# One block load moved ahead of a wait, zero fills cut into eight pieces, and ScalarE's first steps reordered in a fused gated-recurrence and mixture-of-experts kernel

## The reference

```python
x = x + layernorm(attn(layernorm(x)))   # gated recurrence, 4 heads of 64
x = x + layernorm(ffn(layernorm(x)))    # 16 experts, each token goes to the best 4

# attn: gates = (x @ W_in.T) @ W_gate.T + b_gate, split per head into i, f, o, c
c = sigmoid(f) * c + exp(i) * tanh(c_t)                 # scan over the 256 tokens
h = sigmoid(o) * tanh(c * rsqrt(mean(c*c) + eps) * rms_w)
y = h @ W_out.T

# ffn: logits = x @ router.T + bias; softmax over the best 4
out = sum over chosen experts: score * (((up + 1) * gate * sigmoid(1.702 * gate)) @ down_e + bias_e)
```

## Time and profile before

| | us |
|---|---|
| time before, median of 3 runs | 754.29 (753.38 to 758.72) |
| span of the profiled execution | 764.0 |
| first gates of block 0 / of block 1 on PE | 21.35 / 41.34 |
| first scatter on GpSimd | 132.51 |
| last scatter of block 5 issued | 315.58 |
| first transpose of the expert tiles | 323.13 |

### The profile page before, as it was taken

The page is one execution under the profiler, slowest core; times in us unless marked ns, Lnnn a source line. Parts: engine busy times, 40 slices in busy tenths (PEclk is TensorE's granted clock), DMA queues, the critical chain, the costliest instruction groups (busy, mean ns, idle before and its releaser), DMA issues.

```text
span 764.0 us, 13518 instructions
## 1 busy us (share of the span) xinstructions
PE 649.2 (85%) x3800; PEld 419.4 (55%) x3800; DVE 517.9 (68%) x1478; ACT 460.7 (60%) x929; POOL 392.4 (51%) x299
## 2 busy tenths in 40 slices
PE   5989999789979957398999999999999999983460
PEld 2444656465646636355666666666666666651240
DVE  3616587768858887877777777777777777730893
ACT  2676895637656545356677777777777777740242
POOL 0002223333466677646767787566666656665122
PEclk9989998979979976589999999999999999995555
DMA  7965872789532323556977677667766767745997
GB/s 246 421 264 95 166 126 38 177 297 346 175 118 97 121 93 120 151 133 108 181 162 156 124 129 123 108 106 112 112 108 102 119 99 107 111 56 70 350 178 110
DMA packets 111207, 114.86 MB, mean 150 GB/s; under 512 B 31426, under 2 KB 100818, under 8 KB 109474
## 3 DMA queue, kind: packets, MB, share of 16 engines
q0 software_dynamic: 35312, 50.22, 38.6%
q1 hardware_dynamic: 75826, 63.79, 27.9%
HBM read 54.94 MB, written 59.03 MB: 149 GB/s over the span
## 4 chain that ended last, share of the span: by engine, by line
PE 63%; DMA 14%; DVE 10%; ACT 5%; issue 5%; POOL 2%; SPq 0%; POOLq 0%; ACTq 0%; DVEq 0%
DMA routed<-arena,small 9%; PE PS L671 8%; PE PS L672 8%; PE PS L673 8%; PE PS L522 8%; PE PS L660 4%; PE PS L691 4%; PE PS L679 4%; PE PS L692 4%; PE PS L693 4%; DMA sums<-arena 3%; PE PS L555 2%; PE PS L547 2%; PE PS L531 2%; DVE small L1435 1%
## 5 line engine op out<-in xcount | busy, mean ns | idle before, releaser
L1020 POOL DMA_INDIRECT sums<-arena x143 | 223.9, 1566 | 115.6 <-DMA sums<-arena 52.3
L988 POOL DMA_INDIRECT routed<-arena,small x104 | 113.9, 1096 | 84.4 <-DMA routed<-arena,small 70.2
L1406 DVE TENSOR_SCALAR arena<-PS,small 128x256 f32<-128x256 f32 x143 | 77.8, 544 | 90.2 <-ACT arena L945 67.2
L522 PE MATMUL PS<-arena 128*128 128x512 f32 x256 | 131.8, 658 | 5.6 <-ACT arena L745 4.9
L945 ACT ACTIVATE arena<-PS,small 128x256 f32<-128x256 f32 x143 | 67.8, 474 | 99.2 <-PE PS L673 79.1
L745 ACT ACTIVATE arena<-PS 128x512 f16<-128x512 f16 (+1 forms) x179 | 104.5, 591 | 32.7 <-PE PS L500 13.0
L671 PE MATMUL PS<-W,arena 128*128 x286 | 109.4, 383 | 0.2 <-DVE arena L1408 0.2
L672 PE MATMUL PS<-W,arena 128*128 x286 | 109.4, 383 | 0.0
L673 PE MATMUL PS<-W,arena 128*128 x286 | 109.2, 382 | 0.0
L522 PEld LDWEIGHTS PS<-arena 128*128 128x128 f32 x256 | 51.2, 211 | 59.2 <-issue 56.1
L691 PE MATMUL PS<-W,arena 128*128 x286 | 78.1, 273 | 5.0 <-DVE arena L1396 4.8
(11 more groups left out here) (181 smaller groups left out, 1061.1 us busy)
## 6 DMA issues: line engine op xcount, KB each, us to landing
arena<-routed SPq DMA_DIRECT2D x143, 128.0 KB
W<-w_gu SPq DMA_DIRECT2D x8, 1024.0 KB, 23.4
W<-neg_mem POOLq DMA_DIRECT2D x16, 512.0 KB, 8.5
sums<-zero SPq DMA_DIRECT2D x2, 4096.0 KB
W<-sums SPq DMA_DIRECT2D x16, 512.0 KB, 8.8
X<-x SPq DMA_DIRECT2D x8, 512.0 KB, 4.8
W<-w_dn SPq DMA_DIRECT2D x4, 1024.0 KB, 11.3
out<-X SPq DMA_DIRECT2D x8, 512.0 KB
```

What stands on the lines that cost most here:

```text
L522: last = mm(PS[:, 2 + c % 2, :], WcT[:, k, c * P:(c + 1) * P], xT[:, k, :], start=(k == 0), stop=(k == KT - 1))
L988: pool.indirect_dma_start(routed, bass.IndirectOffsetOnAxis(ap=idx, axis=0), rows[b][:, jk // TOPK, :], None).then_inc(rows_sent[lane], 16)
L1020: pool.indirect_dma_start(sums[j % SUMS], bass.IndirectOffsetOnAxis(ap=dst[j % MU], axis=0), yb[u], None, compute_op=ALU.add).then_inc(y_s ...
L1406: L.send(v.tensor_scalar(up[j % 2], acc[:, FF:2 * FF], gu_hi, gu_lo, ALU.min, ALU.max))
```

## The change

- SyncE runs ring_x(6) together with ring_x(5), ahead of the wait for the accumulating DMAs and of the bias load.
- The two zero fills of 4 MB become eight of 1 MB (`clear(n)`), each behind a wait for a count of gate chunks: (5,5), (5,7), (6,1), (6,5), (6,7), (7,1), (7,5), (7,7). The stores of blocks 3, 4 and 5 stand between them, and the spare fills come behind the last one. GpSimd's wait counts eight fills.
- ScalarE evacuates one quarter of WcT, then normalizes block 0, then evacuates the other three quarters. PE's first transposes wait for two quarters, and its gates for all four.
- Squares: five in place of eight in step 0 (two in place of six ahead of `evac_x(1)`), three more at (1,0), (1,1), (1,2); the `w_gu` squares follow: five in step 1 (before: seven), seven in step 2 (before: five), four in step 3 (as before).
- The first two conversions go from (1,4), (1,6) to (1,6), (1,7). `peak_row(1)`, `peaks(0)` and `scales(1)` move later within step 1.

```diff
+ZPARTS = 4
+ZERO_AT = ((5, 5), (5, 7), (6, 1), (6, 5), (6, 7), (7, 1), (7, 5), (7, 7))
-CONV_DN = ((1, 4), (1, 6), (2, 2), (2, 4), (2, 6), (3, 2), (3, 4), (3, 6))
+CONV_DN = ((1, 6), (1, 7), (2, 2), (2, 4), (2, 6), (3, 2), (3, 4), (3, 6))
-SQUARE_AT = (((0, 4),) * 2 + ((0, 5),) * 2 + ((0, 6),) * 2 + ((0, 7),) * 2
-             + ((1, 2), (1, 3), (1, 3), (1, 5), (1, 5), (1, 7), (1, 7))
-             + ((2, 0),) + ((2, 4),) * 3 + ((2, 5),) + ((3, 0),) + ((3, 4),) * 3)
+SQUARE_AT = (((0, 4), (0, 6)) + ((0, 7),) * 3 + ((1, 0), (1, 1), (1, 2))
+             + ((1, 3), (1, 5), (1, 5), (1, 7), (1, 7))
+             + ((2, 0),) * 2 + ((2, 4),) * 3 + ((2, 5),) * 2 + ((3, 0),) + ((3, 4),) * 3)
...
-            ring_x(XRING)
+            for b in range(XRING, XRING + 2):
+                ring_x(b)
             sp.wait_ge(minus_done, 16 * E)
...
-            for a in range(SUMS):
-                sp.dma_start(sums[a][0:TOKENS, :].rearrange("(n p) d -> p n d", p=P),
-                             zero[:, :].unsqueeze(1).to_broadcast([P, NTILE, DIM])).then_inc(zero_sent, 16)
+            def clear(n):
+                a, lo = divmod(n, ZPARTS)
+                rows_n = TOKENS // ZPARTS
+                sp.wait_ge(gate_mm, CHUNKS * ZERO_AT[n][0] + ZERO_AT[n][1])
+                sp.dma_start(sums[a][rows_n * lo:rows_n * (lo + 1), :].rearrange("(n p) d -> p n d", p=P),
+                             zero[:, :].unsqueeze(1).to_broadcast([P, NTILE // ZPARTS, DIM])).then_inc(zero_sent, 16)
+            store_x1(NBLK - XRING)
+            for n in range(3):
+                clear(n)
+            store_x1(NBLK - XRING + 1)
+            for n in range(3, 6):
+                clear(n)
+            store_x1(NBLK - XRING + 2)
+            for n in range(6, SUMS * ZPARTS):
+                clear(n)
...
-            for t in range(NBLK - XRING, NBLK):
+            for t in range(NBLK - XRING + 3, NBLK):
                 store_x1(t)
...
-                    if (s, c) in ((1, 2), (4, 0)):
+                    if (s, c) in ((1, 4), (4, 0)):
                         peaks(s // 4)
...
-            pe.wait_ge(wc_copy, 4)
+            pe.wait_ge(wc_copy, 2)
             transposes_x(0)
             pe.wait_ge(kb_ready, 1)
+            pe.wait_ge(wc_copy, 4)
...
+            evac_wc(0, 0)
             act.wait_ge(r1_ready, 1)
             norm_x(0)
+            evac_wc(0, 1)
+            evac_wc(1, 0)
+            evac_wc(1, 1)
             evac_x(0)
...
-                if s == 1:
-                    peak_row(1)
                 if s == 4:
                     scales(0)
...
                 if s == 1:
-                    scales(1)
+                    peak_row(1)
...
+                if s == 1:
+                    scales(1)
                 if old:
                     choose(s - 2)
                 if s >= 1:
                     low()
```

More of the change, by code:

```diff
@@ L439, in _ @@
                          bias_mem.rearrange("(o e) x -> o e x", o=1)).then_inc(bias_in, 16)
-            for b in range(XRING + 1, NBLK):
+            for b in range(XRING + 2, NBLK):
                 ring_x(b)
             sp.wait_ge(zero_ready, 1)
-            for a in range(SUMS):
-                sp.dma_start(sums[a][0:TOKENS, :].rearrange("(n p) d -> p n d", p=P),
-                             zero[:, :].unsqueeze(1).to_broadcast([P, NTILE, DIM])).then_inc(zero_sent, 16)
+            def clear(n):
[13 more added lines that the diff above has]
+                clear(n)
             spare = routed[PAD0:PAD0 + SPARE * P, :].rearrange("(k p) d -> p k d", p=P)
@@ L745, in copy, with evac_wc @@
                 return nc.scalar.activation(o, i, ACT.Copy, **kw)
[L747 to L750, removed]
+            def evac_wc(n, m):
+                act.wait_ge(wc_mm, 2 * n + m + 1)
+                copy(WcT[:, m, n * 512:(n + 1) * 512], PS[:, 2 * n + m, :]).then_inc(wc_copy, 1)
             def evac_x(t):
@@ L1015, in _ @@
                 if j == 0:
-                    pool.wait_ge(zero_sent, 16 * SUMS)
+                    pool.wait_ge(zero_sent, 16 * SUMS * ZPARTS)
                 pool.wait_ge(y2_ready, j + 3)
```

## The result

Over 20 runs each, the changed kernel took 761.04 us in the median and the kernel before 755.07: a ratio of 1.0076, 95% interval 1.0054 to 1.0098, or 5.7 us slower. The prediction was 751.6 with a range of 744 to 760. It was 9.4 us short, and the time lies 1 us outside the range. The profiled execution of the changed kernel has a span of 762.0 us and a time of 764.17. That is shorter than the span of 764.0 before, because the profile of the kernel before fell in a long execution: the two spans don't show the loss, and the profiles are read for the places of the waits.

The account below looks back on a forecast made before the run. The later of ScalarE's and PE's line (-8.0, `row_high(7)` at 314.1) and GpSimd's scatters (320.0) was to start the tiles. Scatters decided: -2.7 from span 764.0 gives 761.3, times 0.987 is 751.6 us, range 744 to 760.

Parts of the forecast that it names:

- the start's gain: Step 0: gates start some 3 us sooner, but the first square waits for `w_dn` until 31.7, so 0.
- rms_row: ScalarE, after squares leave step 0 and return in step 1: at 50.0 against 54.56, 4.6 us sooner.
- the load of block 6: Issued ahead of the bias wait, it removes VectorE's wait: -3.1 us, with PE's slow stretch staying.
- no wait in `row_high(3)`: ScalarE no longer waits 4.95 us for scatter(1), and PE's mean square regains 1.6: -6.4 us.
- ScalarE's line: ScalarE's and PE's work through the steps: 8.0 us sooner, with `row_high(7)` at 314.1.
- the price of the zeros on the scatters: GpSimd's scatters lose 22.0 us to 10.6 MB of fills, 2.08 us a MB, as pieces or long fills alike.
- The third rival: Pieces hold GpSimd's scatters up altogether: 3.9 us a MB, +16.6 us, 770.7; chance 0.13.
- steps 0 to 3 (+1.95): Start of the kernel: -4.6 + 5.5 + 1.05, so 1.95 us later, delaying the first scatter by 2.0.
- the conversion: First conversion moved to (1,6): `low()` delays `norm_y` and square(1), PE's clock drops; 6.5 us in all, 5.5 taken.
- the second square at (2,5): It stands ahead of `evac_x(3)`, where PE had no slack: 1.05 us later.
- scatter(5) at 320.0: GpSimd's last scatter before the tiles lands 2.0 us later than 318.0, and `row_high(7)` waits for it.
- the 2.7: Whole span: 2.7 us shorter than 764.0, the start of the tiles being set by GpSimd's scatters.

Follow-up runs that it names:

- a_early: The changed kernel with its eight zero pieces and the spare fills sent before any scatter: ratio 0.9995 to the kernel before.
- a_look2: The changed kernel, unchanged, profiled once more: span 760.3 us, tiles from 325.92.
- s_after: The changed kernel with only the first 66 of 143 tiles: median 574.11 us, ratio 0.7616 to the whole kernel before.
- a_look1: The changed kernel, unchanged, profiled once more: span 754.2 us, tiles from 323.41.
- a_low: The changed kernel with step 1's `low()` on VectorE moved behind the product's statistics: ratio 1.0021 to the kernel before.
- b_early: The kernel before with block 6's load moved and zero pieces and spare fills sent before any scatter, ScalarE's order untouched: ratio 0.9946 to the kernel before.
- short kernels: Kernels cut to the first 66 of 143 tiles: before 569.33 us, changed 574.11, before with only ScalarE's reordering 571.13, before with only the zero pieces 573.00.
- b_look1: The kernel before, unchanged, profiled once more: span 753.0 us, tiles from 323.86.
- b_look2: The kernel before, unchanged, profiled once more: span 753.0 us, tiles from 324.67.
- e_act: The kernel before with only the reordered start, squares, conversions, peaks and scales: ratio 1.0065 to the kernel before.
- s_act: The kernel before with only the reordered start, squares, conversions and scales, and only 66 of 143 tiles: median 571.13 us, ratio 0.7594 to the whole kernel before.
- s_blook1: The kernel before with only 66 of 143 tiles, profiled once more: 567.52 us, tiles at 319.02.

## Why the prediction was wrong

**Right, within 0.5 us:** the start's gain is worth nothing because of `w_dn`; `evac_x(1)` at 36.59 (said: 36.5); `rms_row` at 50.45 (50.0); `norm_y`'s wait of 3.63 (3.8) behind `low()`; PE's idle time of over 5 us at the second mean square (6.25) and its 3.57 us at half clock; the load of block 6 worth 7.22 - 3.85 = 3.4 (3.1), with the slow stretch still there; no wait in `row_high(3)`; the tiles behind a scatter in `row_high(7)`. What ScalarE's line alone would give, 314.1, is the 314.12 of `a_early`; that fit is in part luck, since steps 0 to 3 came later than the 314.1 had them.

**About right, the price of the zeros on the scatters:** 100.0 us for 48 scatters, against 48 x 1.605 = 77.0, is 23.0 us for 10.6 MB, 2.17 us a MB (2.08 was taken). Against the same 48 scatters without fills it is more: in `a_early` they take 282.44 - 197.40 = 85.0 us, of which 11.95 are waits for slots, and 100.0 - 73.1 = 26.9 us would be 2.5 us a MB, past the 2.33 at which the prediction turned slower. The third rival's 3.9 did not come, though a wait of 4.19 in `row_high(6)`, a small one of the kind that was its sign, did. The rule of the Trainium skill on whole packets ("DMA: Bandwidth & Descriptors", section "Queues, rings and completion order") was weighed for that rival. Whether a scatter waits for a whole piece is not settled here: a piece lands 4.5 to 5.1 us behind its issue, and beside the one issued at 225.97 GpSimd's next scatter had to wait until 231.72.

**Failed, steps 0 to 3 (+1.95):** the first scatter came 4.97 later. The rows split this. At `rms_row` the kernel is 4.1 us sooner (4.6 said). At the end of the second mean square it is 2.3 later (79.14 + 3.57 = 82.71, before 78.46 + 1.95 = 80.41): the conversion cost 6.4, where the sum had worked out 6.5 and taken 5.5. At the filler matmuls ahead of step 3's mean square it is 3.2 later (110.25, before 107.09): the stretch with the second square at (2,5) cost 0.9 (1.05 said). The other 1.8 come later in step 3, and the sum had no term for them; it had a slow clock at one mean square alone. PE's timeline of the kernel before:

```profile
107.09 1.04 PE L507 MATMUL PS<-KB 128*128 128x256 bf16 x8
...
116.27 0.28 PE L537 MATMUL PS<-K,small 128*16 128x128 f32 x1 [2.51 <-DVE small L1046]
...
117.13 2.56 PE L547 MATMUL PS<-small,K 16*128 16x128 f32 x16
```

PE idles 2.51 us there in both kernels, but in the changed one it then runs at 0.50 (1.2 GHz) to 128 and beyond, and `rms_spread` takes 3.78. The kernel before had 0.83 from 124 to 128, and `rms_spread` took 2.56. This part is a matter of the execution: three more profiles with the changed kernel's order in steps 0 to 3 (`a_look2`, `a_early`, `s_after`) have the first scatter at 137.1 to 137.4, `a_look1` at 133.04. `a_low` shows that the wait of `norm_y` itself goes through to the tiles, 3.7 us of 3.9.

**Failed, scatter(5) at 320.0:** it landed at 322.06 + 2.45 = 324.5. Of the 4.5 us, 3.0 are the late first scatter and 1.5 the 96 scatters (184.6 instead of 183.1). The step's reason, "GpSimd never waited for VectorE's slots before block 6, so it has no idle time in which to take this up", holds for the changed kernel, whose scatters wait for no slots either (1.9 us in `a_look1`, nothing in its other two profiles), but it misread the kernel before: `a_early` shows 12 us of such waits (5.12 + 3.93 + 2.90) once nothing else is late. In the kernel before they were covered by the lateness that the long fills had caused. Fills beside blocks 0 and 1 have that idle time behind them; the pieces, sent beside blocks 2 to 4, leave less of it. So the same bytes cost the end of the line 16.9 us as pieces (322.06, against 305.21 in `a_early`) and 11.1 as long fills (315.58, against 304.52 in `b_early`).

**Failed, the base:** the forecast's -8.0 for ScalarE's line, with -6.4 for the wait in `row_high(3)`, and with it the start of the tiles that the 2.7 were taken from, came out of one execution. Where that wait is full, the profiles have tiles from 323.9 to 326.3, and the changed kernel's 323.4 to 326.3 lies within 3 us of that; where it is 0 or 0.62, they start at 319.0 and 319.2, and it is 4 to 7 us later. The timed loss of 5.7 would fit a mixture of the two. The short kernels, whose times follow the start of the tiles, agree with that; no profile of a whole kernel before shows the second kind. Scaling the span by 0.987 hid that the excess of the first profile lay not in the steps but in the scatter-adds, as `b_look1` and `b_look2` show. It is luck that the changed kernel's span of 762.0 lies 0.7 us from the forecast's 761.3: its tiles start 4.5 us later than forecast, and its adds take 3.0 us less than in the profile of before.

**Open:** why the line of scatter-adds ends 10 to 20 us behind PE from one execution to the next; how often the whole kernel before runs without the wait in `row_high(3)` (four profiles of it all have one); through what ScalarE's order alone loses time, since both profiles of it (`e_act`, `s_act`) have an early first scatter; and the split of the loss between ScalarE's order and the pieces, 0.65 and 0.48% in whole kernels, 4.6 and 6.2 us in short ones.

## What to carry to other kernels

Where two lines race to one place, a wait at their meeting is a matter of the execution: look for it in a second profile before it is priced. A queue's idle time further on is hidden while the queue is late, so work moved along it is priced by what stands behind the new place, and not by bytes alone. Fills that nobody needs yet go where the limiting queue is not yet running: here, ahead of the first scatter, with `low()` behind the statistics, that made 0.9930 of what the move beside the scatters turned into 1.0076.

## What the hardware showed beyond that

The same idle time of PE costs differently. After 2.51 us of it in step 3 the granted clock from 124 to 128 was 0.50 in the changed kernel, 0.83 in the kernel before, and 1.00 in `s_blook1`. The stops end at 119.43, 116.27 and 116.79; at equal distance behind them, 6 to 8 us, the clock was 0.50, 0.50 and 1.00, and 8 to 10 us behind them 0.50, 0.74 and 1.00. The Trainium skill ("TensorE: Matmul & The Clock Gate", part "The HAM clock gate") says that the gate looks at activity on a beat of its own that does not start with the kernel. The rows agree in that the same stop is followed by slow stretches of three lengths; the beat itself no row shows.

An earlier dip can even pay. In `e_act` PE ran at a clock of 0.86 from 112 to 116 and so reached the same wait later; PE's timeline:

```profile
113.75 5.38 PE L523 MATMUL PS<-arena 128*128 128x512 f32 x8
119.94 0.28 PE L538 MATMUL PS<-K,small 128*16 128x128 f32 x1 [0.81 <-DVE small L1051]
120.80 2.05 PE L548 MATMUL PS<-small,K 16*128 16x128 f32 x16
```

It idled 0.81 instead of 2.51 us, kept the full clock behind it (2.05 instead of 3.78 for `rms_spread`), and its first scatter came at 133.10 in place of 137.48, though its step 3 was 0.5 us later there (filler matmuls at 110.76). The same goes for `a_look1`, with a clock of 0.82 in that stretch and the changed kernel's one early first scatter, at 133.04, and for `s_act`, with 0.66 and 132.25.
